# One masked sum in two halves: moving the steps of a top-16 merge between other VectorE work

## The reference

```python
dist = _pairwise_distance(p)                     # 3136 x 3136 per image
_, nn_idx = jax.lax.top_k(-dist, K)              # K = 16 nearest points of each point
nbr = pts[bidx, nn_idx]
e = pts @ W_emb + b_emb
e_n = nbr @ W_emb + b_emb
cat = jnp.concatenate([jnp.broadcast_to(e[:, :, None, :], e_n.shape), e_n], axis=-1)
logits = jax.nn.leaky_relu(cat @ W_att + b_att, negative_slope=0.1)
attn = jax.nn.softmax(logits, axis=2)            # over the 16 neighbours
agg = jnp.sum(nbr * attn, axis=2)
y = jnp.concatenate([pts, agg], axis=-1) @ W_conv + b_conv
```

## Time and profile before

| what | us |
|---|---|
| three executions, median | 11979.92 |
| three executions, lowest and highest | 11979.1 and 11986.17 |
| span of the profiled execution | 11977.8 |

### The profile page before, as it was taken

How to read it: one execution, slowest core, us unless ns; L and a number is a source line. 1 busy time by engine, 2 the same in 40 slices (tenths; PEclk the granted TensorE clock), 3 DMA queues, 4 the chain that set the end, 5 groups by cost and what they waited for, 6 DMA issues and landing times. The chain is left out here.

```text
span 11977.8 us, 322272 instructions
## 1 busy us (share of the span) xinstructions
PE 8919.8 (74%) x114746; PEld 6368.8 (53%) x114746; DVE 10276.0 (86%) x23897; ACT 10163.3 (85%) x11576; POOL 3199.6 (27%) x2040
## 2 busy tenths in 40 slices
PE   2885667777777777877777777777777777777775
PEld 2664345555555555555555555555555555545553
DVE  1000599999999999999999999999999999999997
ACT  2332489999999999999999998999999999989986
POOL 0221022222222222222222222222222222222221
PEclk9887889999999999999999999999999999999998
DMA  9666800000000000000000000000000000000003
GB/s 164 172 177 175 256 16 17 17 17 16 17 17 17 17 17 16 5 17 17 17 17 16 17 17 16 16 17 16 17 17 4 17 17 17 17 16 16 17 4 132
DMA packets 267542, 480.57 MB, mean 40 GB/s; under 512 B 196964, under 2 KB 197348, under 8 KB 248356
## 3 DMA queue, kind: packets, MB, share of 16 engines
q1 hardware_dynamic: 242532, 349.99, 12.5%
q0 software_dynamic: 23424, 109.21, 2.9%
HBM read 353.59 MB, written 105.50 MB: 38 GB/s over the span
## 5 line engine op out<-in xcount | busy, mean ns | idle before, releaser
L843 POOL TENSOR_TENSOR masked<-masked,shares_a 128x784 f32<-128x784 f32 x1600 | 2988.8, 1868 | 7371.9 <-DVE rest L1159 4237.3
L1088 DVE MAX8 found<-scores 128x8 f32<-128x224 f32 x11200 | 3479.0, 370 | 223.7 <-ACT scores L990 188.9
L1017 ACT ACTIVATE turned_sb<-psum 128x512 f32<-128x512 f32 (+1 forms) x5600 | 2945.5, 572 | 507.7 <-PE psum L896 431.4
L898 PE MATMUL psum<-ident_a,masked 128*128 128x128 f32 x19200 | 2649.4, 282 | 902.8 <-ACT turned_sb L1017 860.9
L898 PEld LDWEIGHTS psum<-ident_a,masked 128*128 128x128 f32 x19200 | 2373.5, 195 | 1359.9 <-issue 1359.5
L1127 DVE CUSTOM_DVE_ANT_0 masked<-masked,scores 128x3136 f32<-128x3136 f32 x800 | 2719.1, 3399 | 0.2 <-DVE scores L1119 0.2
L990 ACT ACTIVATE scores<-psum 128x1568 f32<-128x1568 f32 x1600 | 2375.1, 1484 | 224.7 <-DVE minus_top L1127 190.0
L1002 ACT ACTIVATE masked<-masked,minus_top 128x3136 f32<-128x3136 f32 x800 | 2363.5, 2954 | 0.0
L982 ACT ACTIVATE masked<-shares_a,own 128x3136 f32<-128x3136 f32 x800 | 2328.4, 2910 | 1.0
L896 PE MATMUL psum<-ident_a,masked 128*128 128x128 f32 (+1 forms) x10400 | 1764.5, 284 | 528.7 <-ACT turned_sb L1017 494.1
L896 PEld LDWEIGHTS psum<-ident_a,masked 128*128 128x128 f32 (+1 forms) x10400 | 1106.7, 139 | 1289.1 <-issue 1213.3
(11 more groups left out here) (137 smaller groups left out, 6415.4 us busy)
## 6 DMA issues: line engine op xcount, KB each, us to landing
w_in<-in_L_conv_weight_dram POOLq DMA_DIRECT2D x392, 144.0 KB, 3.4
w_in<-in_L_conv_weight_dram SPq DMA_DIRECT2D x392, 144.0 KB, 3.5
points<-unit SPq DMA_DIRECT2D x128, 392.0 KB
shares_a<-share SPq DMA_DIRECT2D x32, 1568.0 KB
windows<-xg SPq DMA_DIRECT2D x42, 928.0 KB, 13.5
xg<-padded SPq DMA_DIRECT2D x32, 406.0 KB, 16.8
table<-table_sb SPq DMA_DIRECT2D x32, 404.2 KB
rows<-table SPq DMA_DIRECT2D x32, 396.0 KB
```

What stands on the lines that cost most here:

```text
L843: nc.gpsimd.tensor_tensor(m, m, shares[:, t.half, k * width:(k + 1) * width], ALU.add).then_inc(logits_ready, 1)
L898: last = nc.tensor.matmul(out, block, ident[:], start=True, stop=True)
L1017: nc.scalar.activation(turned_sb[0:high, t.par, g * GROUP:g * GROUP + width // P, :].rearrange("p a b -> p (a b)"), ps[0:high, bank:bank + ...
L1088: n = step(nc.vector.max(found[:, t.par, c, :], scores[:, t.par, c * PART:(c + 1) * PART]))
```

## The change

`mask` becomes two operations. `mask_low` covers the first half of the columns and leaves its minimum in `low_top`. `mask_high` covers the second half and starts its running minimum from `low_top`, so that `minus_top` is the same as before. `mask_low` signals a new semaphore, `low_masked`; ACT's first copy of scores waits for it and no longer for the whole mask, and the second copy waits for the whole mask. `merge` is cut into its six steps, and `mask_high`, `normalise` and `invert_total` stand between them.

```diff
@@ -690,6 +690,7 @@
         found = enter(nc.sbuf_tensor("found", [P, 2, PARTS, H8], FP32))
         rest = enter(nc.sbuf_tensor("rest", [P, PARTS * H8], FP32))
         weight8 = enter(nc.sbuf_tensor("weight8", [P, PARTS, H8], FP32))
+        low_top = enter(nc.sbuf_tensor("low_top", [P, 2], FP32))
         best = enter(nc.sbuf_tensor("best", [P, NEIGHBOURS], FP32))
         bound = enter(nc.sbuf_tensor("bound", [P, 2], FP32))
         bound_low = enter(nc.sbuf_tensor("bound_low", [P, 2], FP32))
@@ -730,6 +731,7 @@
         doubts_made = enter(nc.semaphore("a_doubts_made"))
         doubts_in = enter(nc.semaphore("a_doubts_in"))
         barred = enter(nc.semaphore("a_barred"))
+        low_masked = enter(nc.semaphore("a_low_masked"))
         masked_ready = enter(nc.semaphore("a_masked"))
         inverse_ready = enter(nc.semaphore("a_inverse"))
         inverse_made = enter(nc.semaphore("a_inverse_made"))
@@ -986,7 +988,10 @@
 
                 act.wait_ge(scored, t.count(SCORED, SCORED_FREE + PER * (quad + 1)))
                 if used is not None:
-                    act.wait_ge(masked_ready, used.count(1, MASKED_FREE + 1))
+                    if quad == 0:
+                        act.wait_ge(low_masked, used.count(1, 1))
+                    else:
+                        act.wait_ge(masked_ready, used.count(1, MASKED_FREE + 1))
                 nc.scalar.activation(scores[:, t.par, quad * QUAD:(quad + 1) * QUAD].rearrange("p (a b) -> p a b", b=SCH),
                                      ps[:, 0:PER * BANK].rearrange("p (a b) -> p a b", b=BANK)[:, :, 0:SCH],
                                      ACT.Copy).then_inc(scores_in, 1)
@@ -1035,7 +1040,7 @@
                 if older:
                     copy_inverse(older, tile(SUM_LAG + 1))
                 if coming:
-                    copy_scores(coming, 1, None)
+                    copy_scores(coming, 1, tile(1))
                 if past:
                     copy_turned(past, 2)
                     copy_turned(past, 3)
@@ -1119,13 +1124,20 @@
                 nc.vector.scalar_tensor_tensor(high, high, bound[:, 0:1], shares[:, t.half, POOL_COLS:N],
                                                ALU.subtract, ALU.min).then_inc(barred, 1)
 
-            def mask(t):
+            def mask_low(t):
 
                 gate(dve, logits_ready, t.count(2, 2), dve_passed)
                 gate(dve, barred, t.count(1, 1), dve_passed)
-                m = masked[:, t.ring, :]
-                nc.vector.tensor_tensor_reduce(m, m, scores[:, t.par, :], -1.0, -NEVER, ALU.add, ALU.min,
-                                               minus_top[:, t.ring:t.ring + 1]).then_inc(masked_ready, 1)
+                m = masked[:, t.ring, 0:POOL_COLS]
+                nc.vector.tensor_tensor_reduce(m, m, scores[:, t.par, 0:POOL_COLS], -1.0, -NEVER, ALU.add, ALU.min,
+                                               low_top[:, t.par:t.par + 1]).then_inc(low_masked, 1)
+
+            def mask_high(t):
+
+                gate(dve, low_masked, t.count(1, 1), dve_passed)
+                m = masked[:, t.ring, POOL_COLS:N]
+                nc.vector.tensor_tensor_reduce(m, m, scores[:, t.par, POOL_COLS:N], -1.0, low_top[:, t.par:t.par + 1],
+                                               ALU.add, ALU.min, minus_top[:, t.ring:t.ring + 1]).then_inc(masked_ready, 1)
 
             def invert_total(t):
                 dve.wait_ge(exp_ready, t.count(1, 1))
@@ -1141,36 +1153,64 @@
                 nc.vector.tensor_tensor(agg[:, t.group_par, at:at + P], ps[:, SUM_BANK:SUM_BANK + P], inverse_sb[:],
                                         ALU.mult).then_inc(agg_ready, 1)
 
-            def merge(t, n):
-
-                found_all = found[:, t.par, :, :].rearrange("p a b -> p (a b)")
-                last = best[:, NEIGHBOURS - 1:NEIGHBOURS]
+            last = best[:, NEIGHBOURS - 1:NEIGHBOURS]
+
+            def found_of(t):
+                return found[:, t.par, :, :].rearrange("p a b -> p (a b)")
+
+            def top_first(t, n):
+
                 dve.wait_ge(chain, n)
-                n = step(nc.vector.max(best[:, 0:H8], found_all))
+                return step(nc.vector.max(best[:, 0:H8], found_of(t)))
+
+            def drop_first(t, n):
+
                 dve.wait_ge(chain, n)
-                n = step(nc.vector.match_replace(rest[:], best[:, 0:H8], found_all, NEVER))
+                return step(nc.vector.match_replace(rest[:], best[:, 0:H8], found_of(t), NEVER))
+
+            def top_second(n):
+
                 dve.wait_ge(chain, n)
-                n = step(nc.vector.max(best[:, H8:NEIGHBOURS], rest[:]))
+                return step(nc.vector.max(best[:, H8:NEIGHBOURS], rest[:]))
+
+            def lower_bound(n):
+
                 dve.wait_ge(chain, n)
-                n = step(nc.vector.scalar_tensor_tensor(bound_low[:], over[:], last, margin[:], ALU.mult, ALU.subtract))
+                return step(nc.vector.scalar_tensor_tensor(bound_low[:], over[:], last, margin[:], ALU.mult, ALU.subtract))
+
+            def set_bound(n):
+
                 dve.wait_ge(chain, n)
-                n = step(nc.vector.scalar_tensor_tensor(bound[:], under[:], last, bound_low[:], ALU.mult, ALU.min))
+                return step(nc.vector.scalar_tensor_tensor(bound[:], under[:], last, bound_low[:], ALU.mult, ALU.min))
+
+            def count_above(t, n):
+
                 dve.wait_ge(chain, n)
-                nc.vector.scalar_tensor_tensor(rest[:], found_all, bound[:, 1:2], weight8[:].rearrange("p a b -> p (a b)"),
+                nc.vector.scalar_tensor_tensor(rest[:], found_of(t), bound[:, 1:2], weight8[:].rearrange("p a b -> p (a b)"),
                                                ALU.is_ge, ALU.mult, accum_out=above[:, 0:1]).then_inc(doubt_ready, 1)
 
             def body(tile):
-                here, coming = tile(0), tile(-1)
+                here, coming, passed = tile(0), tile(-1), tile(1)
                 if here:
                     n = search(here, 1)
-                if tile(1):
-                    mask(tile(1))
+                if passed:
+                    mask_low(passed)
                 if here:
-                    merge(here, n)
+                    n = top_first(here, n)
+                if passed:
+                    mask_high(passed)
+                if here:
+                    n = drop_first(here, n)
                 if tile(NORM_LAG):
                     normalise(tile(NORM_LAG))
+                if here:
+                    n = top_second(n)
                 if tile(3):
                     invert_total(tile(3))
+                if here:
+                    n = lower_bound(n)
+                    n = set_bound(n)
+                    count_above(here, n)
                 if coming:
                     search(coming, 0, 0, 2)
                 if here:
```

## The result

The changed kernel takes 12055.55 us (median of four runs, 12031.0 to 12065.4); the kernel before took 11979.51 beside it (four runs, 11975.9 to 11986.17). The ratio is 1.0062, with a 95% interval from 1.0047 to 1.0077: slower by 0.6%, where I had forecast no change. The profiled execution of the changed kernel has a span of 12029.2 us, 51.4 more than that of the earlier trace rows.

What follows compares the result with a forecast made beforehand. Plain tiles were taken as bound by the loop of ACT and PE, DVE close behind. Plain tiles add nothing, doubt tiles 2.7: span 11977.8 + 2.7 = 11980.5, median 2.1 above, told as 11982 us; range 11956 to 12004.

Steps and rivals of the forecast that it cites:

- The price of the halves: Mask on DVE: two halves at 1.76 us each instead of 3.33 whole, +0.19 us a tile.
- the three covered waits: DVE's merge: waits after first MAX8, MATCH_REPLACE and second MAX8 are covered by other work, each saving 0.11 us.
- DVE's way through the new order: DVE, mask's start to next search: 5.26 us instead of 5.36, net -0.10 a tile.
- count_above at 5.00: DVE: count_above starts 5.00 us after the mask's start instead of 4.82, 0.18 later.
- the plain tile at full clock: ACT's first copies of scores in plain tiles stay 12.53 us apart, set by the loop of ACT and PE.
- the early release that PE takes back: Doubt tiles: ACT's first copy starts 1.57 us earlier, but its second then waits 2.60 us for PE instead of 0.85.
- the moved count: Plain tiles: count_above's 0.18 us delay reaches PE's second scores, but 1.09 us before ACT takes them cover it.
- the "Nothing" for plain tiles: Plain tiles gain nothing: DVE arrives 0.10 us earlier at a copy that ACT has not made.
- The doubt tiles: 15 tiles where the doubt branch runs on DVE: 15 x 0.18 = 2.7 us cost, between 0 and 7.
- rival 1: Early release of ACT's first copy pays in the doubt tiles: 24 us faster, 11956; chance 0.05.
- rival 2: DVE sets the pace of plain tiles after all: -80 us, 11900; chance 0.04.
- rival 3: Mask halves make DVE the bound, its loop passing 12.53 us: 40 to 104 us slower, 12020 to 12084; chance 0.06.

Runs made afterwards that it cites:

- e11: Changed kernel with multiply and reciprocal back behind the count, both mask halves unseeded, a small minimum joining them behind the count: 12072.3 against 11997.56 us, ratio 1.0060.
- e2: Kernel before, mask whole, with the multiply and the reciprocal moved ahead of the whole merge: 12083.11 us, ratio 1.0079 to the kernel before.
- e12: Kernel before, mask whole, with the reciprocal ahead of the merge and a second, unread reciprocal beside it: 12081.33 against 11997.56 us, ratio 1.0064.
- e9: Changed kernel with eight unread products in PE's stop in three tiles of four: 11921.92 against 11984.72 us for the kernel before, ratio 0.9950.
- e10: Kernel before with eight unread products in PE's stop in three tiles of four: 11924.19 against 11984.72 us without them, ratio 0.9948.
- e3: Changed kernel with ACT's first copy of scores waiting for the whole mask again: 12071.3 us, ratio 1.0070 to the kernel before.
- e8: Kernel before, mask whole, with only the reciprocal moved ahead of the merge: 12001.41 against 11984.72 us, ratio 1.0013.
- e1: Changed kernel with the multiply and the reciprocal back behind the count; halves and early release stay: 12054.52 against 11982.51 us, ratio 1.0065.

## Why the prediction was wrong

**What held.** The price of the halves (3.48 for 3.52 us), two of the three covered waits (0.11 and 0.13 us), DVE's way through the new order (6048.66 - 0.24 - 6043.07 = 5.35 us, less the 0.08 by which neighbours overlap: 5.27 from the mask to where the next search could start, forecast 5.26; within it the halves are 0.04 shorter and the start of the second half 0.08 later than forecast), count_above at 5.00, the plain tile at full clock (12.51 us), and the early release that PE takes back. Where I had set the Trainium skill ("VectorE: DVE Perf Modes", section "The DRAIN you can't avoid") against the rows, the rows were right for two steps of three: behind MATCH_REPLACE and the second MAX8 the covered steps did get shorter. The third, in front of the second half, got 0.03 us shorter. I had given the second half's wait for the first one's minimum no term; in e11, where that half has neither the wait nor the seed, it starts 6040.87 - 6040.68 = 0.19 us behind the MAX8, the forecast's figure.

**The step that failed** is the one on the moved count: "In a plain tile PE finishes those scores at 6024.39 + 0.35 = 6024.74 and ACT takes them at 6025.83, so 1.09 us cover it". As a latency it is covered: at full clock ACT's tile stays at 12.51. But I asked only whether somebody waits for what comes behind the count, and not what it does to PE that PE waits longer in front of it. PE's stop grew from 1.19 to 1.36 us in the median, and behind long stops PE's clock falls. So the "Nothing" for plain tiles was wrong by some 46 us of span, about 38 of them in tiles at the lower clock. e2, e12 (the count later, the rest as before: 12083.11 and 12081.33) and e9 with e10 (stop filled: no difference left) show it.

**What led there.** I took the tile's time from three tiles at full clock, and read nothing of those that take longer. The kernel before already had 64 slow tiles of 13.25 us: 64 x (13.25 - 12.50) = 48 us that no term of mine held, and that the eight idle products get back (11984.72 - 11924.19 = 60.5 and 11991.73 - 11922.33 = 69.4 us of the median). A mean clock of 0.952 over a kernel with a busy PE said that there was something.

**The terms that were off in size.** The doubt tiles cost 5.5 us with the tiles behind them, and not 2.7; in the tile shown ACT's waits grow by 12.98 - 12.77 = 0.21, near the 0.18 of the forecast, so the rest lies in what follows, and was not taken apart.

**The rivals.** None was it. The early release pays nothing (rival 1; e3). DVE didn't set the pace (rival 2). The halves were not dear (rival 3): its range of 12020 to 12084 holds the time that came, but by another mechanism, since DVE waits for ACT more than before. The result is right for no case of mine, and the 0.06 that I gave to slower was for a cause that did not happen.

**What stays open.** Why only some of the long stops are followed by a fall: 15 of 54, 39 of 194, 77 of 210. The length of the one stop does not decide it alone: in e8 the clock fell behind stops of 1.15 us, too. Runs of one kernel differ in it too: six runs of e1 go from 12046.19 to 12103.43 us.

## What to carry to other kernels

Moving an instruction that releases PE is priced twice: as a latency, and as the time for which PE stands still in front of it. Look in the trace before for the stops of PE behind which the clock has fallen, count the stops that are nearly as long, and compare a tile behind a fall with one at full clock before you take a tile's time from three rows. If stops of this kind are there, products that nobody reads, put in front of PE's wait, can be a cheap cure. Here eight of them made the kernel before 0.5% faster (11924.19 against 11984.72), and with them the move cost nothing (11921.92); two made the changed kernel 0.3% faster than the kernel before.

## What the runs showed of the hardware

- PE's granted clock fell to its lower level behind some of its stops of 1.35 us and more, in a kernel whose PE is busy 74 to 75% of the span; behind none of the 473 and 265 stops under 1.35 us in the traces before and after, but in e8 behind five of 1.15 us. The Trainium skill ("TensorE: Matmul & The Clock Gate", section "A second HAM failure mode: psum-queue depth-cycling") tells of a kernel whose PE idles briefly and often, and whose clock swings between two levels; the rows here agree, and give a price: 2.13 us for the pair of falls shown.
- A half of the masked sum with a running minimum over 1568 columns takes 1.77 us with a constant as its seed, 1.85 with a seed from memory (e11, the second half without it: 1.77); the whole of 3136 took 3.40.
- An f32 product of 128x128 with the identity is two instructions and took about 0.26 us at full clock: the eight idle ones (16 instructions) took 2.02 us in PE's stop, the four at L900 (8 instructions) 1.06.
